# A gated cross-attention and int8 layer on one core: x loaded transposed, and the order of the work per attention slot rewritten

## The reference, cut to what matters

```python
# per batch; 16 heads of 32
h = layernorm(x)                                # no weights, eps 1e-5
q, k, v = h @ Wq + bq, ctx @ Wk + bk, ctx @ Wv + bv
o = softmax(q k^T / sqrt(32)) v                 # per head
x1 = x + tanh(g_xattn) * (o @ Wo + bo)
z = layernorm(x1)
s = max(amax(|z|, row), 1e-6) / 127
u = (round(z / s) as int8 @ weight_q^T) * s * weight_scale + bias
out = x1 + tanh(g_ffn) * u
```

## Time and profile before

| | before |
|---|---|
| median of 3 runs | 986.92 us (986.37 to 989.01) |
| the profiled execution | 985.63 us |
| its span, first to last instruction | 983.8 us |
| mean granted clock of PE | 0.967 |
| instructions | 18945 |
| PE, DVE, ACT, POOL busy | 889.7, 596.6, 495.0, 382.5 us |
| DMA | 59.59 MB, mean 61 GB/s |

### The profile page before, as it was taken

One profiled execution on the slowest core, in us unless ns is written; L12 is line 12 of the kernel. 1 busy time (PEld: TensorE's weight loads), 2 busy tenths in 40 slices (PEclk: granted clock), 3 DMA queues, 4 the chain that ended last, 5 costly groups with the idle time before them and its releaser, 6 DMA issues.

```text
span 983.8 us, 18945 instructions
## 1 busy us (share of the span) xinstructions
PE 889.7 (90%) x7718; PEld 572.5 (58%) x7776; DVE 596.6 (61%) x985; ACT 495.0 (50%) x694; POOL 382.5 (39%) x389
## 2 busy tenths in 40 slices
PE   2787899999999999999999999999999999988874
PEld 1564566565656666565756666565756666553442
DVE  3455448576675758576675748576675848373524
ACT  3235346464654646464654646464655646353522
POOL 0004125344345425344344435344344435253633
PEclk9988899999999999999999999999999999997886
DMA  5312020120303030120303030120303020101011
GB/s 167 141 59 86 2 88 15 55 76 33 112 23 108 23 107 18 58 73 31 115 22 108 22 111 14 54 77 27 119 23 108 17 71 1 58 30 58 29 44 43
DMA packets 32854, 59.59 MB, mean 61 GB/s; under 512 B 4224, under 2 KB 4864, under 8 KB 32768
## 3 DMA queue, kind: packets, MB, share of 16 engines
q1 hardware_dynamic: 32768, 58.38, 18.2%
HBM read 41.59 MB, written 16.78 MB: 59 GB/s over the span
## 4 chain that ended last, share of the span: by engine, by line
PE 64%; DVE 17%; ACT 9%; issue 8%; DMA 1%; SPq 0%; POOL 0%; POOLq 0%; ACTq 0%; DVEq 0%
PE bank_a L243 30%; PE pv_ps L311 5%; PE sum_ps L313 5%; PE scores L298 5%; PE bank_b L269 4%; DVE row_max L694 4%; DVE u_sb L751 3%; PE scores L281 3%; PE bank_a L263 3%; PE bank_b L249 3%; DVE cen L744 2%; DVE on L710 2%; PE bank_b L263 2%; DVE q_top L732 2%; ACT q_hi L523 1%
## 5 line engine op out<-in xcount | busy, mean ns | idle before, releaser
L533 ACT ACTIVATE probs<-scores 120x2048 f32<-120x2048 f32 x64 | 120.3, 1880 | 91.5 <-PE scores L302 91.5
L889 POOL TENSOR_TENSOR o_lo<-on,o_hi 128x512 fp32r<-128x512 f32 x64 | 81.9, 1280 | 187.9 <-ACT o_hi L549 187.9
L694 DVE TENSOR_REDUCE row_max<-scores 128x16 f32<-128x1920 f32 x64 | 137.5, 2149 | 2.3 <-PE scores L281 2.1
L885 POOL TENSOR_TENSOR x<-x,gbo_r 128x512 f32<-128x512 f32 x64 | 81.9, 1290 | 129.9 <-DMA x<-in_x 129.9
L243 PE MATMUL bank_a<-wo_hi,o_hi 128*128 128x512 f32 x256 | 109.5, 428 | 4.9 <-POOL o_lo L889 2.5
L243 PE MATMUL bank_a<-xt_hi,wq_hi 128*128 128x512 f32 x256 | 107.6, 420 | 6.8 <-DVE q_lo L682 5.1
L898 POOL TENSOR_TENSOR x<-x,u_sb 128x512 f32<-128x512 f32 x64 | 82.1, 1283 | 73.8 <-DVE u_sb L751 73.8
L682 DVE SCALAR_TENSOR_TENSOR q_lo<-bank_a,bq_c,q_hi 128x512 fp32r<-128x512 f32 x64 | 48.0, 749 | 91.7 <-ACT q_hi L523 91.7
L243 PE MATMUL bank_a<-xt_lo,wq_hi 128*128 128x512 f32 x256 | 101.8, 398 | 0.0
L243 PE MATMUL bank_a<-wo_lo,o_hi 128*128 128x512 f32 x256 | 101.7, 397 | 0.0
L243 PE MATMUL bank_a<-xt_hi,wq_lo 128*128 128x512 f32 x256 | 101.5, 396 | 0.0
(11 more groups left out here) (89 smaller groups left out, 1730.0 us busy)
## 6 DMA issues: line engine op xcount, KB each, us to landing
x_in<-in_x SPq DMA_DIRECT2D x64, 256.0 KB, 3.5
x<-in_x SPq DMA_DIRECT2D x64, 256.0 KB, 5.9
out_x<-x SPq DMA_DIRECT2D x64, 256.0 KB, 2.1
ctx_sb<-in_ctx_t SPq DMA_DIRECT2D x8, 360.0 KB, 5.5
probs<-in_wq SPq DMA_DIRECT2D x1, 1024.0 KB, 7.1
x<-in_wo SPq DMA_DIRECT2D x1, 1024.0 KB, 9.9
wk_sb<-in_wk SPq DMA_DIRECT2D x1, 768.0 KB, 8.6
wv_sb<-in_wv SPq DMA_DIRECT2D x1, 768.0 KB, 7.6
```

Of the source, the lines that this page charges most:

```text
L533: act.activation(probs[0:KEYS], scores[0:KEYS], ACT.Exp, scale=SCALE).then_inc(p_ready, 1)
L694: dve.tensor_reduce(row_max[:].rearrange("p (t r) j -> p r t j", r=ROWG)[:, :, :, j], scores[:, :, 0:QT * KEYS].rearrange("p r (t k) -> p ...
L885: pool.tensor_tensor(x1[n % 2][:, t], x1[n % 2][:, t], gbo_r[:], ALU.add).then_inc(xb_ready, 1)
L889: pool.tensor_tensor(o_lo[:, j], on[j % 2][:], o_hi[:, j].bitcast(F32), ALU.subtract).then_inc(o_split, 1)
```

## The change

- **x.** SP also loads `x_t`, x transposed on the host, into `xt` (1 MB a batch). POOL's `scale_x` multiplies it by a row of rstd; `high_x` and `low_x` split it in place of the PSUM transposes. `turn_x`, `normalise` and the shift are gone. The mean of x is taken out by centring the columns of Wq on the chip once (`wq_mean`: PE averages, DVE subtracts). rstd comes per token on partitions, and is needed as a row on all partitions: SP stores it to DRAM (`store_rstd`) and loads it back broadcast (`load_rstd`). `x_in` shrinks to two tiles. Token order in `x_v` and `out_v` becomes (t p).
- **Keys and values** are made in three split passes; ctx, Wk and Wv are split on the chip, ctx once per pair.
- **Order.** Each quarter of a step has one output projection and one query projection. q(n, 0) is made in step n-2, q(b, 1..3) in the step before b's attention (q has a ring of five). The second half of the int8 layer of a batch runs one step later (e = i-2). `turn_z` and `copy_zt` take two tiles at once, into one whole bank; `quantised_layer` for t = 1 goes to `pv_ps`. `turn_max` is the last but one of the step, in `bank_a`.
- **Buffers.** `x1` is one batch (the last batch uses `xt`), `u_sb` one tile, `on` four, `v_sb` three, ctx one.
- **Ahead and behind** are lists of their own: the first projects batch 0 and q(1, 0) with `scores`, `sum_ps` and `pv_ps` as extra banks; the last gives each output projection of batch 15 a bank. Steps run for i = 0 to 15. Some first loads are issued by ACT.

The diff, cut to its core:

```diff
-        x_in = sb("x_in", [P, QT, D])
...
+        x_in = sb("x_in", [P, 2, D])
...
-        x1 = [sb(f"x1_{i}", [P, QT, D]) for i in range(2)]
...
+        x1 = sb("x1", [P, QT, D])
...
             def load_x(n, t):
+                if n > 1 or t >= 2:
+                    sp.wait_ge(x_stats, nth(n, QT, t) - 2)
+                load(x_landed[t % 2], x_in[:, t % 2], x_v[n, t])
+
+            def load_xt(n):
                 if n > 0:
-                    sp.wait_ge(xn_ready, nth(n - 1, QT, t))
-                load(x_landed[t], x_in[:, t], x_v[n, t])
+                    sp.wait_ge(x_split, nth(n - 1, DT, 3))
+                load(xt_landed, xt[:], x_t[n])
+
+            def store_rstd(n):
+                sp.wait_ge(x_pool, nth(n, 2, 1))
+                sp.dma_start(rstd_v[n % 2], ln_rstd[:], allow_slow_non_contiguous=True).then_inc(rstd_stored, 16)
+
+            def load_rstd(n):
+                sp.wait_ge(rstd_stored, 16 * (n + 1))
+                if n > 0:
+                    sp.wait_ge(x_scaled, nth(n - 1, DT, 3))
+                load(rstd_landed, rstd_b[:], rstd_rows[n % 2].partition_broadcast(P))
 
             def load_residual(n, t):
-                if n >= 2:
-                    sp.wait_ge(out_stored[n % 2][t], 16 * (n // 2))
...
+                elif n > 0:
+                    sp.wait_ge(out_stored[t], 16 * n)
...
-            def turn_x(n, t, bank):
-                pe.wait_ge(xn_ready, nth(n, QT, t))
-                for c in range(DT):
-                    ins = pe.transpose(bank[:, c * P:(c + 1) * P], xn[t % 2][:, c * P:(c + 1) * P], ident_f[:])
-                ins.then_inc(x_turned, 1)
...
             def project_k(pair, j, bank):
...
                 for c in range(CT):
-                    ins = pe.matmul(bank[:, 0:KEYS2], wk_sb[:, c, j * P:(j + 1) * P], ctx_sb[pair % 2][:, c],
-                                    start=c == 0, stop=c == CT - 1)
+                    ins = three(bank[:, 0:KEYS2], (wk_hi[:, c, cols], wk_lo[:, c, cols]), (ctx_hi[:, c], ctx_lo[:, c]),
+                                c == 0, c == CT - 1)
                 ins.then_inc(k_done, 1)
...
             def project_v(n, bank):
...
+                    ins = three(bank[0:KEYS, :], (ctx_hi[:, c, keys_of(n)], ctx_lo[:, c, keys_of(n)]),
+                                (wv_hi[:, c], wv_lo[:, c]), c == 0, c == CT - 1)
                 ins.then_inc(v_done, 1)
...
+            pe.wait_ge(consts_ready, 4)
+            pe.wait_ge(wq_landed, 16)
+            for c in range(DT):
+                ins = pe.matmul(pv_ps[:], mean_of, wq_stage[:, c], start=c == 0, stop=c == DT - 1)
+            ins.then_inc(wq_mean, 1)
...
+            def low_x(n, c):
+                dve.wait_ge(xt_hi_done, nth(n, DT, c))
+                dve.tensor_tensor(xt_lo[:, c], xt[:, c], xt_hi[:, c].bitcast(F32), ALU.subtract).then_inc(x_split, 1)
...
             def dequantise(m, t, bank):
                 dve.wait_ge(ffn_done, nth(m, QT, t))
-                if m > 0 or t >= 2:
-                    dve.wait_ge(out_ready, nth(m, QT, t) - 2)
...
+                if m > 0 or t > 0:
+                    dve.wait_ge(out_ready, nth(m, QT, t) - 1)
...
+            def scale_x(n, c):
+                pool.wait_ge(rstd_landed, 16 * (n + 1))
+                pool.wait_ge(xt_landed, 16 * (n + 1))
+                pool.tensor_tensor(xt[:, c], xt[:, c], rstd_b[:], ALU.mult).then_inc(x_scaled, 1)
```

More of the change, by code:

```diff
@@ L21 @@
 BANK = 512
+QRING = 5
 LN_EPS = 1e-5
@@ new lines, in _ @@
+            for t in range(QT):
+                load(x0_landed[t], x0_stage[:, t], x_v[0, t])
+            load(wq_landed, wq_stage[:], rows(wq))
+            load_xt(0)
+            load(bq_landed, bq_c[:], bq)
+            load(bv_landed, bv_r[:], bv.partition_broadcast(P))
+            load_x(1, 0)
+            load_x(1, 1)
+            store_rstd(0)
+            load_rstd(0)
+            load(ident_landed, ident_f[:], consts_f32)
+            sp.wait_ge(x_stats, nth(0, QT, 3))
+            load(wo_landed, wo_stage[:], rows(wo))
@@ L205, in _ @@
+            load_x(1, 2)
+            load_x(1, 3)
+            sp.wait_ge(wq_lo_done, DT)
+            load(wv_landed, wv_stage, rows(wv))
+            store_rstd(1)
+            load_xt(1)
+            load_rstd(1)
+            load(rest_landed, u_sb[:].bitcast(I32), rows(wq8))
             load(rest_landed, gbo_r[:], bo.partition_broadcast(P))
@@ L237, in _ @@
+            for t in range(1, QT):
+                store(B - 2, t)
+            for t in range(QT):
+                store(B - 1, t)
+            for t in range(QT):
+                sp.wait_ge(out_stored[t], 16 * B)
         @block.tensor
@@ new lines, in step @@
+                if is_batch(m):
+                    if is_batch(e):
+                        pe.wait_ge(u_ready, nth(e, QT, 2))
+                    else:
+                        pe.wait_ge(x1_ready, nth(m, QT, 0))
+                    project_o(m, 1, bank_a)
+                attend(i, 1)
+                if is_batch(n):
+                    if is_batch(e):
+                        pe.wait_ge(u_ready, nth(e, QT, 3))
+                    else:
+                        pe.wait_ge(q_split, nth(b, DT, 1))
+                    project_k(pair, k0, bank_b)
@@ L404, in step @@
+                scores_by_key(i, 2)
                 if is_batch(m):
@@ new lines, in _ @@
+            pe.wait_ge(x1_ready, nth(e, QT, 3))
+            quantised_layer(e, 2, bank_a)
+            project_o(m, 3, scores[:, 3])
+            quantised_layer(e, 3, sum_ps)
+            turn_z(m, 0, bank_b)
+            pe.wait_ge(u_ready, nth(e, QT, 2))
+            quantised_layer(m, 0, bank_a)
+            pe.wait_ge(u_ready, nth(e, QT, 1))
+            quantised_layer(m, 1, pv_ps)
+            turn_z(m, 1, scores[:, 0])
+            pe.wait_ge(u_ready, nth(m, QT, 0))
+            quantised_layer(m, 2, bank_a)
@@ L504, in _, with load @@
+            pe.wait_ge(u_ready, nth(e, QT, 3))
+            quantised_layer(m, 3, sum_ps)
         @block.scalar
         def _(act):
-            def normalise(n, t):
-                act.wait_ge(x_pool, nth(n, 4, 3))
-                act.activation(xn[t % 2][:], x_in[:, t], ACT.Identity, scale=ln_rstd[:, t:t + 1],
-                               bias=ln_shift[:, t:t + 1]).then_inc(xn_ready, 1)
-            def high_x(n, t, bank):
-                act.wait_ge(x_turned, nth(n, QT, t))
-                act.activation(xt_hi[:, :, t * P:(t + 1) * P], bank[:].rearrange("p (c s) -> p c s", c=DT),
-                               ACT.Copy).then_inc(xt_hi_done, 1)
+            def load(landed, dst, src):
+                act.dma_start(dst, src).then_inc(landed, 16)
@@ L599, in step @@
-                if is_batch(n):
                     high_k(pair, k1, bank_a)
-                    high_x(n, 3, bank_b)
                 if is_batch(m):
@@ L761, in step @@
                     x1_statistics(m, 0)
-                if is_batch(n):
-                    low_x(n, 0, bank_b)
                 if is_batch(b):
-                    maxima(b, 1)
-                if is_batch(i):
-                    normalise_o(i, 0)
+                    maxima(b, 0)
+                normalise_o(i, 0)
+                if is_batch(b):
+                    low_q(b, 1, bank_b)
+                if is_batch(e):
+                    dequantise(e, 2, bank_a)
+                if is_batch(f):
+                    x_statistics(f, 1)
+                if is_batch(e):
+                    dequantise(e, 3, bank_b)
                 if is_batch(m):
@@ L787, in step @@
                     quant_round(m, 1)
-                if is_batch(i):
-                    normalise_o(i, 1)
+                if is_batch(b):
+                    low_q(b, 2, bank_b)
+                if is_batch(f):
+                    x_statistics(f, 2)
+                if is_batch(m):
+                    residual(m, 2, bank_a)
+                    x1_statistics(m, 2)
+                    quant_max(m, 2)
                 if is_batch(b):
                     maxima(b, 2)
+                normalise_o(i, 2)
+                if is_batch(b):
+                    low_q(b, 3, bank_b)
+                if is_batch(m):
+                    dequantise(m, 0, bank_a)
+                if is_batch(n):
+                    for c in range(DT):
+                        low_x(n, c)
+                if is_batch(f):
+                    x_statistics(f, 3)
                 if is_batch(m):
```

907 lines of the change are left out of this document (499 added, 408 removed).

## The result

| | before | after |
|---|---|---|
| median, us | 986.8 (986.4 to 989.0, 4 runs) | 1047.9 (1046.0 to 1049.2, 4 runs) |
| ratio to before | 1 | 1.0613 [1.0589, 1.0636] |
| profiled execution: span, us | 983.8 | 1046.4 |
| mean granted clock | 0.967 | 0.91 |

The forecast was 905 us, with a range of 878 to 950. The kernel is slower than before by 61 us, and 98 above the end of the range.

The account below looks back on a forecast made before the run. PE's own work was taken to bound the middle, not the edges. Twelve full steps saving 45.6 us and edges saving 35.8, together 81.4, gave a span of 902.4 and a time of 905 us, range 878 to 950.

Parts of the forecast that it names:

- The store of rstd in 3 us: Store of 512 rstd values to DRAM each step: 3 us, between 2.1 and 8.0, free up to about 6.5.
- rival 1: Row of rstd or reload of x1 comes late by 3 us a step: +36, 941 us; chance 0.13.
- Against: DMA at a fifth: Argument against a late rstd row or x1 reload: the DMA engines are busy only a fifth of the time.
- The lock at no cost: DVE and POOL locking each other out over SBUF: weighed for low_x, but given no cost in the sum.
- Rival 3: DVE's four low_x a step locked out by POOL: 2.8 us a step, +34, 939 us; chance 0.09.
- Keys, values and transposes: PE work in a full step: x transposes gone -1.9 us, keys in split passes -0.7, values -0.5.
- Rival 2: Split keys don't get cheaper, 4.2 us instead of 2.1, over 13 steps: +28, 933 us; chance 0.08.
- The full step of 51.6: Each of twelve full steps falls from 55.4 to 51.6 us by PE's work and waits, 45.6 us in all.
- Step 0 in 46 us: First step, with 34.5 us of PE work where it had 44.5: 46 us, -7.7.
- The sign: Whole kernel: faster 0.95, same 0.02, slower 0.03.
- rival 5: Slower than before: x1's tile store and reload in series hold POOL, DVE and PE; 1009 us if both take 9.9; chance 0.03.
- The last step and tail: From the last turned maxima to the end: last step 39.6 us (-6.8), tail 33 us (-4.3).

Follow-up runs that it names:

- b: The changed kernel with rstd stored as 128 rows of 16 bytes instead of 512 pieces of 4, by another token order in the statistics: 976.1 us, 0.9887 of before.
- h: b with POOL's bias_x, bias_x1 and scale_x on 8 columns instead of 512: 922.4 us, 0.9341 of before.
- j: b with integers of tiles 2 and 3 a step later on ACT, low_k and maxima(b, 1) ahead of quant_factors on DVE: 958.4 us, 0.9714 of before.

## Why the prediction was wrong, point by point

The 144 us between the forecast and the span divide by the runs: 74 are the form of the store (after less b), 55 POOL's work and what it holds up (b less h), and 15 remain in h, 10.5 of them in step 0.

- **The store of rstd in 3 us: this step failed.** It took 9.5, and 8.0 had been my bound from above. That bound was 2 KB behind 3 MB of other loads, a transfer that, as I read it, waits for the bytes ahead of it. This one is late because of its pieces: the same 2 KB in 128 rows took 1.4. No row of before showed it. I had the count of 512 from the sentence of the Trainium skill cited in the prediction, and gave it to rival 1 without a price of its own. Even with 9.5 the sum would have been short: I let late rstd cost its excess over 6.5 us, 3 us a step, but the store also doubled x_t's landing on the same queue. Measured 5.4 us a step (after less b), plus 5.3 in the start (7.4 more there are POOL's, b less h), where it took 11.9 us (issued at 11.50, readback at 23.35) for the 9 of my layout, and 2.7 in step 0.
- **"Against: DMA at a fifth" (rival 1): the wrong measure.** The share was a reading of the engines of before; what holds the step is one transfer in an ordered queue.
- **A stall priced by its own length: failed.** PE's wait of 2.6 us a step went with a granted clock of 0.91 to 0.97; a group of products 7 us behind it took 5.24 instead of 2.98 us. b, with two waits of 1.4 and 1.2 us a step, has 1.00 in eleven of its twelve full steps and 0.97 in one, of 56.3 us.
- **The lock at no cost: this step failed too.** The forecast had nothing for it; b less h is 2.9 us a step. Rival 3 had 2.8, which is luck, as it put them on low_x. But low_x is nearly as long in h (0.91 us of mean) as in after (0.97), and h has the 2.9 us back all the same. What h shortens are split_max (1.06 to 0.22 us in the mean), q_top (0.53 to 0.21) and q_mul (0.81 to 0.21) of quant_factors, and quant_round (0.77 to 0.50). The trace of before had it: I looked at quant_round alone, but q_top had a median of 0.81 us there and a shortest of 0.15, and at 264.79 and 276.02 us it ends with the POOL operation beside it:

```profile
L732 DVE TENSOR_TENSOR q_top<-q_amax,x_rstd x32: 148/812/1156, 154.0 to 967.1; 128x2 f32<-128x2 f32 x32
```

  That POOL gained 5.2 us of work I had right (23.6 to 28.4 busy in the step), and asked only whether it fits.
- **Rivals singly.** I gave 941 to the late row and 939 to the lock, and took the range as if one of them at most were true. Both were: 905 + 36 + 34 = 975 would have been above my 950, even with the row too cheap.
- **Keys, values and transposes: right.** L249 of before is gone. In b, at full clock, split passes on 240 columns start at 421.12 and 421.23, 0.11 us apart, the lower end that I took; a group of nine is 1.20 us in j's chain. Rival 2 is refuted. PE's busy time in the full step of b is 51.6 us, of h 50.8.
- **The full step of 51.6: near where nothing holds it**, 51.9 in h, and the start 67.8 for 67, step 1 48.9 for 49.5, step 14 48.2 for 48, end 73.7 for 72.6. h leaves out POOL work that I had counted, so it shows the sum of PE's terms, not that they could be had with POOL's.
- **Step 0 in 46 us: failed in every form of the changed kernel**, 54.6 to 60.3, h included. It has 34.5 us of PE work at full clock by my sum; in h:

```profile
68.00:124.00 56.00, 45.92 (x399) 28.96 (x399) 23.54 (x32) 20.90 (x28) 5.66 (x9) 0.75 0.16 43
```

  PE is busy 45.9 us of 56 at a granted clock of 0.75, against 0.87 in the earlier trace rows. With less work between its waits, the step was done at a lower clock, and I priced only the work taken out. That the lower clock is the cause of all 10 us isn't shown; no run changed it alone.
- **The sign.** Gains of 81 us had to be outweighed by 6.3 us a step; it was 8.6. I had named that for rival 5, by store and reload of x1, and they took 13 us together, not 18.2: the reload was late, but behind scale_x it was not what POOL waited for. What POOL waited for last is rstd's row, held back by its store and by x_t: rival 1.
- **The last step and tail**: 81.2 for 72.6. In b, with the store quick, 82.3; in h 73.7. So the miss there is POOL's too, not the store's.

## What to carry to other kernels

A small transfer can be priced by its pieces, not its bytes (9.5 against 1.4 us for the same 2 KB): lay the data out so that what one partition stores is contiguous (here another order of tokens in the statistics gave 72 us), and where a form of DMA is new, take no bound for it from other forms, and count what stands behind it in its queue. Work moved to an engine that is not the bound still needs a place in the order; before POOL gets more of it, look for DVE's short operations on SBUF that somebody waits for (their shortest, median and longest time show whether they are held), and put them behind those that matter. Rivals that don't exclude each other add, and the range has to hold their sum.
